# Graph attention kernel: queries projected ahead of keys in every step

## The reference

```
eq, nk, nv = lin(x, n2e_q), lin(x, n2e_k), lin(x, n2e_v)
edges = ln(attn(eq, nk, nv, mask=adj.T) + x, norm1)
nq, ek, ev = lin(x, e2n_q), lin(edges, e2n_k), lin(edges, e2n_v)
nodes = ln(x + attn(nq, ek, ev, mask=adj), norm2)
out   = ln(nodes + lin(gelu(lin(nodes, w1)), w2), norm3)
return layernorm(x + out)
```

## Time and profile before

| what | value |
|---|---|
| median of 3 runs | 2907.52 us (2905.23 to 2907.68) |
| the profiled execution's own time | 2905.24 us |
| its span in the profile | 2903.4 us |
| mean granted TensorE clock | 0.995 |
| TensorE busy (matmul) | 98% of the span |
| VectorE, ScalarE, GpSimd busy | 60%, 53%, 38% |
| attention, groups 0 to 31 | from 0 to about 1475 us |
| a group in the steady state | 45.3 us |

### The profile page before, as it was taken

One profiled execution on the slowest core, in us unless ns is written; L12 is line 12 of the kernel. 1 busy time (PEld: TensorE's weight loads), 2 busy tenths in 40 slices (PEclk: granted clock), 3 DMA queues, 4 the chain that ended last, 5 costly groups with the idle time before them and its releaser, 6 DMA issues.

```text
span 2903.4 us, 50564 instructions
## 1 busy us (share of the span) xinstructions
PE 2855.2 (98%) x17920; PEld 2396.3 (83%) x17920; DVE 1743.0 (60%) x5684; ACT 1549.5 (53%) x4138; POOL 1097.0 (38%) x995
## 2 busy tenths in 40 slices
PE   8999999999999999999979999999999999999997
PEld 7888888888788888888868888888888888888886
DVE  7888888888888888888853233332233332233333
ACT  6777777777878888788854222222222222222221
POOL 3443444434455465554603321233321233321233
PEclk9999999999999999999999999999999999999998
DMA  7555555555667676776753110101110101110201
GB/s 201 123 125 122 126 119 124 123 123 124 154 157 175 154 179 178 163 171 154 183 136 109 58 59 30 58 29 58 58 58 29 58 29 58 58 58 29 71 2 58
DMA packets 488013, 296.08 MB, mean 102 GB/s; under 512 B 278912, under 2 KB 410112, under 8 KB 487808
## 3 DMA queue, kind: packets, MB, share of 16 engines
q1 hardware_dynamic: 487808, 293.49, 38.7%
HBM read 159.21 MB, written 67.11 MB: 78 GB/s over the span
## 4 chain that ended last, share of the span: by engine, by line
PE 96%; DVE 2%; DMA 1%; issue 0%; SPq 0%; ACT 0%; POOL 0%; POOLq 0%; DVEq 0%; ACTq 0%
PE proj L871 35%; PE proj L1321 24%; PE score L1335 12%; PE proj L1335 12%; PE score L922 6%; PE att_out L855 5%; PE att_turn L837 2%; DMA ffn_weight_raw<-in_w 1%; DMA att_weight_k_raw<-in_n2e_k_w 0%; DVE ffn_stats L1218 0%; DVE normed L697 0%; DVE weight_k_lo L718 0%; DVE weight_v_lo L718 0%; DVE att_stats L702 0%; DVE att_p_lo L769 0%
## 5 line engine op out<-in xcount | busy, mean ns | idle before, releaser
L1254 DVE TENSOR_TENSOR hidden_lo<-hidden,hidden_hi 128x512 fp32r<-128x512 f32 x256 | 188.1, 735 | 935.0 <-ACT hidden_hi L1106 935.0
L1113 ACT ACTIVATE hidden<-proj,ffn_bias 128x512 f32<-128x512 f32 x256 | 176.6, 690 | 994.9 <-PE proj L1321 994.8
L520 ACT ACTIVATE att_probs<-att_probs,att_minus_max 128x128 f32<-128x128 f32 x1024 | 397.3, 391 | 83.1 <-DVE att_minus_max L760 83.0
L769 DVE TENSOR_TENSOR att_p_lo<-att_probs,att_p_hi 128x512 f16<-128x512 f32 x256 | 211.2, 864 | 153.0 <-ACT att_p_hi L527 153.0
L1173 POOL TENSOR_TENSOR source_lo<-source_raw,source_hi 128x512 fp32r<-128x512 f32 x60 | 79.5, 1325 | 449.5 <-ACT source_hi L1124 449.5
L621 POOL CAST att_v<-att_v_rest 128x512 bf16<-128x512 f32 x128 | 96.6, 754 | 390.3 <-DVE att_v_rest L736 390.3
L760 DVE CUSTOM_DVE_ANT_0 att_probs<-score,att_mask 128x128 f32<-128x128 f32 x1024 | 225.0, 285 | 21.6 <-PE score L922 21.1
L477 ACT ACTIVATE turned<-att_turn,att_shift,att_gain 128x128 f32<-128x128 f32 x512 | 192.9, 458 | 71.9 <-PE att_turn L837 71.8
L871 PE MATMUL proj<-weight_v_hi,source_hi 128*128 128x512 f32 x512 | 215.8, 421 | 7.0 <-DVE weight_v_lo L718 7.0
L636 POOL TENSOR_TENSOR source_lo<-source_raw,source_hi 128x512 fp32r<-128x512 f32 x128 | 163.4, 1300 | 129.9 <-ACT source_hi L543 129.9
L871 PE MATMUL proj<-source_hi,weight_k_hi 128*128 128x512 f32 x512 | 201.5, 393 | 2.6 <-DVE weight_k_lo L718 2.6
(11 more groups left out here) (148 smaller groups left out, 8258.3 us busy)
## 6 DMA issues: line engine op xcount, KB each, us to landing
att_tokens<-in_x SPq DMA_DIRECT2D x128, 256.0 KB, 3.2
edges_t<-turned SPq DMA_DIRECT2D x64, 256.0 KB, 2.7
source_raw<-edges_t SPq DMA_DIRECT2D x16, 1024.0 KB, 6.1
att_query_raw<-in_x_t SPq DMA_DIRECT2D x16, 1024.0 KB, 7.6
nodes_t<-turned SPq DMA_DIRECT2D x64, 256.0 KB, 2.8
source_raw<-nodes_t SPq DMA_DIRECT2D x16, 1024.0 KB, 6.1
normed<-nodes SPq DMA_DIRECT2D x16, 1024.0 KB, 5.6
ffn_weight_raw<-in_x SPq DMA_DIRECT2D x16, 1024.0 KB, 8.1
```

The lines of the kernel that those rows point to most:

```text
L520: nc.scalar.activation(probs[:, j, :], probs[:, j, :], ACT.Exp, bias=minus_max[:, j:j + 1], scale=-1.0, accum_out=row_sum[:, side, j:j + 1 ...
L769: nc.vector.tensor_tensor(p_lo[:, 4 * h:4 * h + 4, :], probs[:, 4 * h:4 * h + 4, :], p_hi[:, 4 * h:4 * h + 4, :], ALU.subtract).then_inc(p ...
L1113: nc.scalar.activation(hidden[:, c % 2, :], up_bank[c % 2][:], ACT.Gelu, bias=bias_1[:, c:c + 1]).then_inc(activated, 1)
L1254: nc.vector.tensor_tensor(hidden_lo[:, c % 2, :], hidden[:, c % 2, :], hidden_hi[:, c % 2, :].bitcast(F32), ALU.subtract).then_inc(hidden_ ...
```

## The change

In every step the queries are projected first and the keys second. ScalarE and VectorE take them in that order too, the places and banks of the two are exchanged, and the scores wait for the place of the keys, which is now the later one. Nothing is added or left out: the same instructions run on the same engines.

```diff
+def query_place(g, u):
+
+    return PROJ * g + 2 + 3 * u - skipped(g, u)
+
+
 def key_place(g, u):
-
-    return PROJ * g + 2 + 3 * u - skipped(g, u)
-
-
-def query_place(g, u):
     return PROJ * g + 3 + 3 * u - skipped(g, u)
...
+    def query_bank(u):
+        return proj_bank[(2 + 3 * u) % PROJ_BANKS]
+
     def key_bank(u):
-        return proj_bank[(2 + 3 * u) % PROJ_BANKS]
-
-    def query_bank(u):
         return proj_bank[(3 + 3 * u) % PROJ_BANKS]
...
+                query_high(g, own, u)
                 key_high(g, own, u)
-                query_high(g, own, u)
...
+                query_low(g, own, u)
                 key_low(g, own, u)
-                query_low(g, own, u)
...
             if h == 0:
-                pe.wait_ge(proj_split, query_place(g, u) + 1)
+                pe.wait_ge(proj_split, key_place(g, u) + 1)
...
+                queries(g, parity, own, u)
                 keys(g, parity, own, u)
-                queries(g, parity, own, u)
```

## The result

The changed kernel takes 2938.5 us (median of 4 runs, 2936.68 to 2940.5) against 2906.38 for the kernel before beside it, a ratio of 1.0109 with a 95% interval of 1.0097 to 1.0121. It is 32 us slower; forecast were 2937 and slower. The profiled execution took 2940.5 us, the slowest of the four, and its span is 2938.7.

A forecast was written before the change was run, and what follows sets the result against it. TensorE, busy 98% of the span, was taken as the bound. Terms 2.8 + 2.75 + 23.3 + 1.1 + 0.9 = 30.85 us gave 2936.1 to 2938.4, forecast 2937 us; 2924 to 2948 held 0.80 of the chances.

The forecast's parts named there:

- What bounds the kernel: Whole kernel: TensorE, busy 98% of the span, sets the end; the question is where it begins to wait.
- The hand-over: Each second-pass group: TensorE waits for GpSimd's low part of the next queries, 15 x 1.55 = +23.3 us.
- The start: First projection: queries wait for the low part of the query weights, which the keys' matmuls covered before; +2.8 us.
- The term of 0.9 for the clock: Before the first queries: TensorE stands still 3.0 us and its clock may fall; half of 1.7 taken, +0.9 us.
- The second pass begins: Group 16: queries start at 746.78 again, but the 12 key matmuls now follow them; +2.75 us.
- The chain on VectorE: Last low part comes 0.55 us later; the two scores that already wait each grow by that, +1.1 us.
- (b): Scores: VectorE's margin of 0.4 doesn't suffice, a wait of 0.3 in 30 groups, 9 more, 2946 us; chance 0.10.
- (a): Hand-overs: the copies aren't delayed and each costs only 0.8, total +19.5, 2926 us; chance 0.08.
- (c): Hand-overs: the clock falls at each of the 15 waits, 25.5 us more, 2962 us; chance 0.07.
- (d): Hand-overs: GpSimd's split is slowed where it is moved, 27 us more, 2964 us; chance 0.05.
- (e): Hand-overs are hidden after all, the other terms stay: +7.5, 2915 us; chance 0.05.
- (f): Whole kernel not slower: scores' waits and half clock give back 6.8 against +5.5, 2906 us; chance 0.03.

The follow-up runs named there:

- the wait alone in the kernel before: Kernel before with only TensorE's wait for the second pass's split queries moved ahead of the keys of step 0; 2924.3 us, ratio 1.0062.
- the two moves of the copies: Changed kernel with ScalarE's four copies of the next queries ahead of `key_high`, 2918.59 us, or behind the turned block's copy as well, 2983.59 us.
- filler: Changed kernel plus 32 unread matmuls on TensorE before it waits for the queries of group 16, 2937.83 us.
- every wait of the second pass mended: Changed kernel with query weights first, two query copies ahead of `key_high` and two behind, and 32 unread matmuls at the pass's start; 2909.63 us, ratio 1.0010.

## Why the prediction was right

**The total.** 31 us more were forecast and 32 measured, and the mechanism is the one forecast. That the totals agree so closely is in part luck. In the profiled run the start cost 1.96 instead of 3.7, the pass's start 1.3 more than forecast, the hand-overs 1.6 more and the last steps 0.5 more, and 2.9 came up in the feed-forward stage that no term held.

**What bounds the kernel**: right. The lag grows at the few places of the table and nowhere else, although every step was reordered.

**The hand-over**: right in mechanism and nearly in size, 1.66 us each against 1.55. That position and ScalarE's order share it, 0.86 and 0.80, is what the wait alone in the kernel before and the two moves of the copies showed. The prediction had 0.7 for the first and 0.85 for the second. It let TensorE's first projection start 1.52 late; it starts 1.56 later behind the scores than before. Two errors in that chain offset each other in part: the copies start 1.41 behind the first half and not 1.35, and GpSimd's four took 5.03 and not 5.06. The miss of 0.11 is mostly the slower matmul behind the wait. The prediction gave it 0.1 and said that 1.55 holds the greater part of it, but 1.55 is only 0.03 above 1.52; measured are 0.10, and the 0.07 between them make 1.1 us of the 1.6 over the 15.

**The start**: the mechanism is shown by the run with the query weights first. The size isn't fixed: the wait was 1.8 to 3.7 us in the traces. ScalarE's first copy of the query weights, which waits for the load, began between 14.91 and 15.86, and TensorE was free for the queries between 15.4 and 16.3. The first query projection came at 18.11 in the changed kernel, not near 18.8. The term of 0.9 for the clock came to nothing there (1.00 over 18 to 24), but in two other runs the clock fell, at the waits of 3.6 and 3.7 us. The forecast's 3.7 for both lies within the 1.96 to 4.53 that came.

**The second pass begins**: this term was mis-sized most. I had written that at 746.78 the half clock is there already, so that the order costs 2.75 only. The wait became 8.1 us in one piece, and the lower clock lasted longer: 0.56 over 6.9 us in the changed kernel, against 0.51 over 3.5 us in the earlier trace rows. The term was 4.09 (3.2 to 3.7 in the other traces without filler), and 4.09 - 2.75 = 1.3 of it go to the clock. The filler took 2.8 away, more than that, since the kernel before loses 1.7 to the clock at the same place. The bound, 1.7 more for the clock, held.

**The chain on VectorE**: 0.44 at each of the two scores against 0.55. The sign that was named for it, waits near 1.5 and 4.8, did not come: they are 0.79 and 4.09. The prediction looked for the delay at the scores alone, and TensorE met it before them, at the turned block and at the values. No experiment takes this term away. The margin of step 2 in a steady group fell from 0.99 to 0.57 where I had said 0.4, and didn't run out, so rival (b) didn't come. It was near: with all copies ahead of the keys the margin was 0.05, and 4.1 us were lost, 2.6 of them there.

**The other rivals.** (a) fell with the 1.40 of idle time in each. (c), the clock at every wait, did not come at 1.4 us and came in 9 of 15 at 3.2 us; the length of the wait was what mattered here, though not it alone, and the prediction's reason, no fall at 0.91 us and in the pair behind 1470, was the right kind of row. (d) didn't come: GpSimd's four pieces took 5.03 against 5.06 before. Only where the copies were moved later still did they take 5.17. (e) and (f) need that the low part be ready in time, and it wasn't. The sign that ScalarE would wait at L514 no longer failed: it waits there 17 times, because a late query projection is late for ScalarE too.

That nothing at all stays of the order itself is shown only in part: with every wait of the second pass mended, the time is still 1.0010 times that before, and the 2 to 3 us are accounted for, in the one trace, by the two scores' waits, the last step and the order at the pass's start. No kernel here is faster than the one before by more than can be measured.

## What to carry to other kernels

Before two stages of a pipeline are exchanged, ask of each what it alone waits for, and who hid that wait. Here the input of one stage came from a side chain over two other engines that ended 0.7 us after the other stage had begun. The trace showed no wait for it at all, since a hidden arrival leaves no row; only the difference between the side chain's end and the other stage's start shows it. Then count what the follower engine now does ahead of that side chain: here that doubled the price, and two small copies moved to where ScalarE had been idle for 0.78 us took all of it back. And look among the waits of the weight loads too: where a margin has gone, they show it before the matmuls do.

## What the runs showed of the hardware

A wait costs TensorE more than its idle time in the profile: 1.66 us for 1.40, and 0.86 for 0.57. Of the difference 0.16 is the last matmul before the wait, which runs out alone, and 0.10 the first one behind it. The clock's fall went with how long the wait was and wasn't the same each time at one length: none in 15 waits of 1.4 us, nine in 15 waits of 3.2 us, each of the nine costing 1.6 us or more on top. Unread matmuls in the wait kept the granted clock at 1.00, and that made the work behind it faster in the trace. Between medians they bought 0.7 to 1.3 us, no more than the runs of one kernel differ by; once that was because a chain over VectorE and ScalarE was the next to be late.
